# Starting the quantised layer's first tiles inside the last turn of the attention before it

## The reference, cut to what matters

```
x = x + tanh(g_xattn[0]) * L0_xattn_ref(layernorm(x), ctx, ...)       # stage a
x = x + tanh(g_ffn[0])   * L0_ffn_ref(layernorm(x), w_gate, w_up, w_down, ln_weight)   # stage b

activation_quant(x):  s = 127 / clip(max|x| of the row, 1e-5);  round(x * s) / s
weight_quant(w):      s = 1 / clip(mean|w|, 1e-5);              clip(round(w * s), -1, 1) / s
bit_linear(x, w):     activation_quant(x) @ weight_quant(w).T
L0_ffn_ref(x):        h = silu(bit_linear(x, w_gate)) * bit_linear(x, w_up)     # 512 -> 2048
                      h = ln_weight * rms_norm(h)
                      return bit_linear(h, w_down)                              # 2048 -> 512
```

## Time and profile before

| | |
|---|---|
| median of 3 runs | 2313.41 us (2310.81 to 2313.84) |
| profiled execution, its own time | 2315.0 us |
| span of that execution, first to last instruction | 2313.3 us |
| TensorE (PE) busy | 2162.3 us, 93% of the span |
| VectorE (DVE) busy | 1305.5 us, 56% |
| ScalarE (ACT) busy | 1078.7 us, 47% |
| GpSimd (POOL) busy | 670.7 us, 29% |
| mean granted clock of TensorE | 0.971 |

### The profile page before, as it was taken

How to read it: one execution, slowest core, us unless ns; L and a number is a source line. 1 busy time by engine, 2 the same in 40 slices (tenths; PEclk the granted TensorE clock), 3 DMA queues, 4 the chain that set the end, 5 groups by cost and what they waited for, 6 DMA issues and landing times. The chain is left out here.

```text
span 2313.3 us, 43017 instructions
## 1 busy us (share of the span) xinstructions
PE 2162.3 (93%) x17901; PEld 1801.3 (78%) x17918; DVE 1305.5 (56%) x2227; ACT 1078.7 (47%) x1882; POOL 670.7 (29%) x679
## 2 busy tenths in 40 slices
PE   6899998699969999999999999999889999899996
PEld 4666676344459999999999999999677877799996
DVE  7666776377764445444444445454454545677774
ACT  4687533377744444333343344333345553415553
POOL 3111110255412222111111111221245453124664
PEclk9999999799989999999999999999889999999998
DMA  6454202100022223222223123221000000247996
GB/s 254 147 184 128 83 2 110 55 1 1 1 109 81 112 92 117 77 108 74 92 92 110 61 69 135 74 83 55 24 1 2 2 2 29 83 173 234 275 281 112
DMA packets 46497, 215.29 MB, mean 93 GB/s; under 512 B 6112, under 2 KB 6112, under 8 KB 31840
## 3 DMA queue, kind: packets, MB, share of 16 engines
q1 hardware_dynamic: 29536, 139.13, 16.6%
q0 software_dynamic: 16768, 73.41, 11.2%
HBM read 169.00 MB, written 43.52 MB: 92 GB/s over the span
## 5 line engine op out<-in xcount | busy, mean ns | idle before, releaser
L231 POOL TENSOR_TENSOR c_prob<-c_prob,c_inv_mass 128x512 f32<-128x512 f32 x128 | 130.4, 1037 | 358.1 <-DVE c_inv_mass L223 358.1
L213 ACT ACTIVATE c_prob<-c_s_ps,c_neg_peak 128x256 f32<-128x256 f32 x256 | 117.8, 473 | 177.8 <-DVE c_neg_peak L205 177.8
L50 PE MATMUL c_ring<-bc_xt,bc_wq_hi 128*128 128x256 f32 x512 | 148.6, 290 | 1.5 <-DVE bc_xt L1972 1.5
L50 PE MATMUL c_ring<-c_ctx,c_w_hi 128*128 128x256 f32 x512 | 145.6, 284 | 1.9 <-DVE c_qt_lo L1964 1.9
L52 PE MATMUL c_ring<-bc_xt,bc_wq_lo 128*128 128x256 f32 x512 | 145.8, 285 | 0.0
L51 PE MATMUL c_ring<-bc_xt,bc_wq_hi 128*128 128x256 f32 x512 | 145.7, 285 | 0.0
L51 PE MATMUL c_ring<-c_ctx,c_w_hi 128*128 128x256 f32 x512 | 143.4, 280 | 0.0
L52 PE MATMUL c_ring<-c_ctx,c_w_lo 128*128 128x256 f32 x512 | 143.0, 279 | 0.0
L1686 POOL DMA_DIRECT2D c_ctx<-kept_scratch x24 | 13.2, 550 | 346.7 <-PE c_ring L52 346.7
L1186 POOL TENSOR_TENSOR b_hw<-b_h,b_lnw 128x512 f32<-128x512 f32 x64 | 80.6, 1271 | 86.7 <-DVE b_h L1354 86.7
L3042 POOL DMA_INDIRECT out<-el_r,e_target x44 | 83.5, 1898 | 74.7 <-DMA out<-el_r,e_target 59.9
(11 more groups left out here) (547 smaller groups left out, 7129.8 us busy)
## 6 DMA issues: line engine op xcount, KB each, us to landing
x_res<-b_w SPq DMA_DIRECT2D x48, 512.0 KB, 4.8
bc_xt<-kept_scratch POOLq DMA_DIRECT2D x24, 1024.0 KB, 5.1
c_ctx<-kept_scratch POOLq DMA_DIRECT2D x24, 1024.0 KB, 5.3
e_raw<-e_w SPq DMA_DIRECT2D x15, 1536.0 KB
bc_raw<-c_w SPq DMA_DIRECT2D x16, 1024.0 KB, 5.3
h_res<-e_w SPq DMA_DIRECT2D x7, 1536.0 KB
kept_scratch<-bc_xt SPq DMA_DIRECT2D x8, 1024.0 KB, 3.9
kept_scratch<-c_ctx SPq DMA_DIRECT2D x8, 1024.0 KB, 3.9
```

The lines of the kernel that those rows point to most:

```text
L50: pe.matmul(out, lhs[0], rhs[1], start=first, stop=False)
L213: ins = act.activation(self.prob[:, u % 2, j, :], self.s_ps[:, j, :], ACT.Exp, bias=self.neg_peak[:, u % 2, j:j + 1], accum_out=self.mass[ ...
L231: pool.tensor_tensor(part, part, self.inv_mass[:, u % 2, js].unsqueeze(2).to_broadcast([P, 2, SEQ]), ALU.mult).then_inc(self.prob_done, 1)
```

## The change

The head of stage b, for pair 0, and the first quarters of tile 0 are issued in turn 7 of stage a.

- A class FirstTiles holds the buffers, semaphores and steps that both Blocks use. Its SBUF buffers (xn, xq, xqt, sg, ident_h, h0, lnw and the small ones) lie over stage a's buffers from ctx_f on, which are not read any more in turn 7. g_ps and u_ps are the four banks of s_ps, and bank 3 also takes the first transposes.
- VectorE, turn 7, behind find_spread_after(6): the cast of the identity, the spread of tiles 0 to 13, xn of tiles 0 and 1, find_x_scales(0). gated(0, 0) ahead of add_to_x(7, 0), find_x_scales(1) ahead of add_to_x(7, 1), gated(0, 1) at the end.
- ScalarE: round_x(0) behind the last exponentials and ahead of output_high(7, 0); copy_x(0) ahead of output_high(7, 1); at the end silu(0, 0), round_x(1), silu(0, 1). The Tanh of stage b's gate moves to the start of stage a.
- TensorE: turn_x(0) between masses(7, 1, 1) and inverses(7, 1); up(0, 0) between inverses(7, 1) and outputs(7, 0); up(0, 1) and up(0, 2) at the end.
- POOL: normalise(1) behind the last output_low. SP: the load of lnw behind the last turned scores; the load of the gate at the start.
- Stage b is left with the spread of tiles 14 and 15, silu(0, 2) and (0, 3), gated(0, 2) and (0, 3), up(0, 3) and all four weight(0, k) on POOL. Tiles 1 to 15 have the order that they had. find_spread and the steps up, turn_x, round_x, copy_x, silu and gated are methods of FirstTiles with the text that they had.

```
 sync
@@
+            sp.dma_start(early.gate_sb[:, :], early_gate).then_inc(early.gate_in, 16)
@@
-            sp.wait_ge(wq_in, 48)
+            sp.wait_ge(st_ready, C * BATCH)
+            sp.dma_start(early.lnw[:, :], early_ln).then_inc(early.lnw_in, 16)
+            sp.wait_ge(early.lnw_in, 16)
 gpsimd, behind the turns
+            early.normalise(pool, 1)
 tensor
+                if i == BATCH - 1:
+                    pe.wait_ge(early.ident_done, 1)
+                    early.turn_x(pe, 0, x_turned)
                 if nxt:
                     scores(i + 1, 0)
...
                 if now:
                     inverses(i, 1)
+                if i == BATCH - 1:
+                    pe.wait_ge(wq_in, 48)
+                    early.up(pe, 0, 0)
...
                 if now:
                     outputs(i, 1)
+            early.up(pe, 0, 1)
+            early.up(pe, 0, 2)
 scalar
+                if i == BATCH - 1:
+                    early.round_x(act, 0)
                 if now:
                     output_high(i, 0)
...
                 if now:
                     output_raw(i, 1)
+                if i == BATCH - 1:
+                    early.copy_x(act, 0, x_turned)
...
+            early.silu(act, 0, 0)
+            early.round_x(act, 1)
+            early.silu(act, 0, 1)
 vector
+            def first_tiles():
+                dve.tensor_copy(early.ident_h[:, :], ident[:, :]).then_inc(early.ident_done, 1)
+                dve.wait_ge(late_stats, TILES - TB)
+                early.find_spread(dve, early_chain, 0, TILES - TB)
+                for t in range(TB):
+                    dve.tensor_scalar(early.xn[:, t, :], x_res[:, t, :], early.agg[:, t, 0:1], early.rstd[:, t:t + 1], ALU.subtract,
+                                      ALU.mult).then_inc(early.xn_done, 1)
+                early.find_x_scales(dve, early_chain, 0)
...
                 if i >= 1:
                     find_spread_after(i - 1)
+                if i == BATCH - 1:
+                    first_tiles()
...
+                if i == BATCH - 1:
+                    early.gated(dve, early.h0[:, early.quarter(0)], 0, 0)
                 if now:
                     add_to_x(i, 0)
+                if i == BATCH - 1:
+                    early.find_x_scales(dve, early_chain, 1)
...
                 if now:
                     add_to_x(i, 1)
             find_spread_after(BATCH - 1)
+            early.gated(dve, early.h0[:, early.quarter(1)], 0, 1)
 stage b, vector
-            dve.tensor_copy(ident_h[:, :], ident[:, :]).then_inc(ident_done, 1)
-            norm_of.find_spread(dve, Chain(dve, norm_of.steps, begun), 0, TILES)
...
+            early.find_spread(dve, chain, TILES - TB, TILES)
+            dve.wait_ge(early.gain_done, 1)
 stage b, gpsimd
-            pool.wait_ge(spread_found, 1)
-            normalise(1)
-            pool.wait_ge(lnw_in, 16)
             for n in range(PERIODS):
...
                 if n % 2 == 1 and tile(n + 3):
-                    normalise((n + 3) // 2)
+                    if n == 1:
+                        pool.wait_ge(spread_found, 1)
+                    early.normalise(pool, (n + 3) // 2)
```

More of the change, by code:

```diff
@@ L92 @@
 INVERSE_SQRT_STEPS = 10
[L95 to L125, removed]
 class Picks:
@@ L277, in output_low, with image_attention @@
         dve.tensor_tensor(to, of, f32(high), ALU.subtract).then_inc(self.o_lo_done, 1)
[L280 removed]
+def image_attention(nc, x_res, ident, begun, x_dram, ctx_t, w_t, rows, gate, handed, picks, early, early_gate, early_ln):
     tag = "a"
@@ L861, in _ @@
             act.activation(gain[:, :], gate_sb[:, :], ACT.Tanh).then_inc(gain_done, 1)
+            act.wait_ge(early.gate_in, 16)
+            act.activation(early.gain[:, :], early.gate_sb[:, :], ACT.Tanh).then_inc(early.gain_done, 1)
             for i in TURNS:
@@ L1127, in quantised_ffn @@
         w_mean = handed.w_mean
[L1128 to L1135, removed]
+        hw, h1 = sb("hw", [P, 2, F]), sb("h1", [P, F])
         hqt = sb("hqt", [P, FC, P], BF16)
[L1137 to L1140, removed]
+        down_gain, sq_sum = sb("down_gain", [P, 1]), sb("sq_sum", [P, 2])
         h_var, h_half, h_rstd, h_tmp, h_all, h_scale = (
@@ L1211, in _ @@
         def _(pe):
-            def turn_x(j):
-                pe.wait_ge(xq_done, j + 1)
-                pe.wait_ge(xqt_done, j)
-                for t in range(TB):
-                    for c in range(C):
-                        mm = pe.transpose(xt_ps[:, c, t, :], low_words(xq[:, t, :], c), ident_h[:, :])
-                mm.then_inc(xt_ready, 1)
-            def up(n, k):
-                if k == 0:
-                    pe.wait_ge(xqt_done, n // 2 + 1)
-                m = n * NB + k
-                for ps, w, free, ready in ((g_ps, w_gate, sg_done, g_ready), (u_ps, w_up, h_done, u_ready)):
-                    if m >= 2:
-                        pe.wait_ge(free, m - 1)
-                    for c in range(C):
-                        mm = pe.matmul(ps[:, k % 2, :], xqt[:, n // 2 % 2, c, n % 2, :], w[:, c, quarter(k)], start=c == 0, stop=c == C - 1)
-                    mm.then_inc(ready, 1)
             def turn_h(n):
@@ L1243, in down @@
                         pe.wait_ge(ht_copied, 2 * n + k // 8 + 1)
-                    mm = pe.matmul(d_ps[:, :], hqt[:, k, :], w_down[:, k, :], start=k == 0, stop=k == FC - 1)
+                    mm = pe.matmul(d_ps[:, :], hqt[:, k, :], early.w_down[:, k, :], start=k == 0, stop=k == FC - 1)
                 mm.then_inc(d_ready, 1)
-            pe.wait_ge(ident_done, 1)
-            turn_x(0)
             for n in range(PERIODS):
-                if tile(n):
-                    up(n, 0)
-                    up(n, 1)
+                if tile(n) and n > 0:
+                    early.up(pe, n, 0)
+                    early.up(pe, n, 1)
                 if tile(n - 2):
@@ L1303, in copy_h @@
                 act.activation(hqt[:, half * FC // 2:(half + 1) * FC // 2, :], ht_ps[:, half], ACT.Copy, bias=-HALF_ONE).then_inc(ht_copied, 1)
-            act.wait_ge(gate_in, 16)
-            act.activation(gain[:, :], gate_sb[:, :], ACT.Tanh).then_inc(gain_done, 1)
-            round_x(0)
-            copy_x(0)
             for n in range(PERIODS):
-                if tile(n):
-                    silu(n, 0)
-                    silu(n, 1)
+                if tile(n) and n > 0:
+                    early.silu(act, n, 0)
+                    early.silu(act, n, 1)
                 if tile(n - 2):
@@ L1415, in _ @@
                     find_scales(n - 1)
-                if n % 2 == 0 and tile(n + 2):
-                    find_x_scales((n + 2) // 2)
+                if n % 2 == 0 and n > 0 and tile(n + 2):
+                    early.find_x_scales(dve, chain, (n + 2) // 2)
                 if tile(n):
```

227 lines of the change are left out of this document (146 added, 81 removed).

## The result

| | before | after |
|---|---|---|
| median | 2313.41 us (2310.81 to 2321.27, 5 runs) | 2296.2 us (2293.49 to 2299.28, 5 runs) |
| ratio to before, 95% interval | | 0.9919 (0.9903 to 0.9935) |
| profiled execution: own time, span | 2315.0, 2313.3 us | 2299.28, 2297.6 us |
| mean granted clock | 0.971 | 0.975 |

The kernel became faster, by 17.2 us by the medians and by 15.0 to 22.4 us by the interval of the ratio; 15.3 had been forecast, as 2298.1 us with a range of 2294.8 to 2302.3. So by this group of runs the forecast lies near the low edge of what was gained.

A forecast was written before the change was run, and what follows sets the result against it. TensorE, busy through most of the span, was taken as the bound, so only its idle stretches pay. Tile 0 through at 442.8 instead of 458.06 saves 15.3 us: predicted median 2298.1 us, range 2294.8 to 2302.3.

The forecast's parts named there:

- all the moved work was hidden: Last attention turn: idle gaps cover the moved work, such as VectorE's 6.7 us chain in 8.35 us idle.
- tile 0's shift: Quantised layer's head: tile 0 through at 442.8 instead of 458.06, 15.3 us sooner, moving all later work.
- the added wait: New block's start: POOL's pair stops VectorE's first short step, adding 2.2 us, bounds 0 and 2.5.
- The clock's term: Output products: high clock, from 425.98; first bank's sum 3.07 us after the first product, the second 2.8 later.
- S: Start of the new block, forecast at 436.3, which is 1.21 us after the last end of the block before.
- The pair of gated products: New block, VectorE: gated(0, 2) and gated(0, 3) at 0.75 us each, ending tile 0 at S + 6.5.
- the way from the first output product to the block's start: End of the attention block: first output product at 425.98, new block at 436.3.
- The reference point: Whole kernel: 15.3 us off the execution's 2315.0 gives 2299.7; less 1.6 to the runs' median, 2298.1.
- the low clock to the end of the outputs: Rival, output products: clock stays low as in the trace; gain 12.4 us, time 2301.0; chance 0.2.
- lost in the first tiles: Rival, first tiles: 3 to 5 us given back; gain 10 to 12 us, time 2302.4; chance 0.07.
- VectorE isn't stopped: Rival, new block's start: POOL doesn't stop VectorE's short steps; gain 17.5 us, time 2295.9; chance 0.2.

The follow-up runs named there:

- after_again: The changed kernel, unaltered, timed a second time: 2300.95 us, ratio 0.9951 to the kernel before.
- pool_held: Changed kernel, with POOL waiting for the spread of tiles 14 and 15 before weight(0, 0): 2299.49 us, ratio 0.9943 to the kernel before.
- the other two groups: The changed kernel, unaltered, in two more groups of runs: 2300.95 us (ratio 0.9951) and 2300.34 us (0.9936).
- gap_filled: Kernel before, plus eight unread bf16 products on TensorE between the last inverses and the outputs: 2313.27 us, ratio 1.0001; second look 2316.32 us.
- up_behind: Changed kernel, with up(0, 0) moved behind the output products and gated(0, 0) to the end of VectorE's block: 2302.83 us, ratio 0.9956.
- gap_turned: Kernel before, plus eight unread float32 transposes on TensorE between the last masses and the inverses: 2310.71 us, ratio 0.9999; second look 2308.5 us.

## Why the prediction came out as it did

The mechanisms were right: all the moved work was hidden, the clock stayed high, the new wait at the block's start is there and is POOL's, tile 0's shift is kept to the next stage (16.5 at tile 0, 16.7 there). The total was right within the scatter of three groups, and too small for the first of them. In the stretch itself 15.3 was forecast and 16.7 came. What failed is the size of two terms of the sum, the start of the outputs and the added wait, and the step by which the sum was turned into a total:

- **The clock's term.** I took the outputs at the high clock but let them start at 425.98, as if the clock had still fallen ahead of them ("it never falls, or is back by 426"). From the reciprocal to the block's end it never fell: the inverses took 1.13 for 1.81 and the outputs start 0.67 sooner after the reciprocal, in all three traces, also in the one (after_again) that like the kernel before's has no low-clock stretch ahead of the reciprocal. The outputs' own way to the second sum was forecast as 5.87 and took 5.77. (By the windows of the earlier trace rows the clock came back at 431.9 in the kernel before, not at 432.1; nothing rests on that.)
- **The added wait.** Forecast S + 5.0 for the first gated product, measured 4.43, so 0.57. The stop cost 1.85 (pool_held) for the 2.2 that I took, and the chain without it 2.58 for 2.8. The stop begins only behind the aggregates, which run beside POOL.
- **The smaller ones.** The pair of gated products took 1.40 for 1.50 and the rest of the layer was 0.23 shorter (203.75 for 203.98 from tile 0 to the next stage); the way from the first output product to the block's start was 10.45 for 10.32. Sum: 15.26 + 0.67 + 0.57 + 0.10 + 0.23 - 0.13 = 16.7, the first trace's 16.70.
- **The reference point.** I set the sum against the median as if the rest of the kernel stood still. It moves by up to 6 us ahead of the stretch and 7 behind it from one execution to another, which the 3 us between the kernel before's first runs hid; the range should have been some 2 us wider at both ends. The first group's ratio fell below its lower end (2294.7 for 2294.8) by such scatter, as far as the record goes; the other two groups gave 11.3 and 14.8 by their ratios, less than the stretch.

The rivals: the low clock to the end of the outputs appeared in none of the changed kernel's traces; nor was anything lost in the first tiles, though TensorE idles 2.48 us there and the clock was low for 3.4 us in one of three traces. "VectorE isn't stopped" was wrong in its mechanism, and its time, 2295.9, is nearest to the first group's median by chance.

What stays open is why the unchanged parts scatter as they do (the low-clock stretches of TensorE fall at other places in each execution, which the traces show, but I didn't test that they are all of it), and why the totals gain less than the stretch: gap_filled's isn't seen in its total at all, and some 2.5 us of the changed kernel's 16.7 aren't either. More traces of the kernel before would tell whether its one trace has a stretch longer than is usual.

## What to carry to other kernels

When work is moved across a block's border, look for what it leaves at the head: here a chain that only the last pair needed stayed in front of the first tile and cost 3.1 us, more than the forecast was off in the stretch (1.4). A filled gap of TensorE can pay twice, for the work and for the clock of what follows. Here it was the gap directly ahead of the outputs that counted: left empty it cost 1.6 us (up_behind), and transposes one gap earlier didn't make up for it (gap_turned). Judge a change of less than 1% by a stretch between two marks in several traces, of the kernel before as well as of the changed one, and then see whether the totals agree.

## What was not expected of the hardware

- A short VectorE step beside a POOL product stood twice in a row, 1.00 and 1.19 us, once for each POOL product of 1.27, while the aggregates (0.25 for two) and the gated products, which read one operand from PSUM, weren't stopped at all. After the pair had ended, nine steps of 0.16 ran undisturbed.
- The same sequence, from the sum that ends the turn before to the last turn's first reciprocal, took 10.4 us in five of the fourteen traces and 11.8 in nine, by a low-clock stretch of 3.4 us in the middle of it; nothing between.
